# A ViT tower with attention, two scans and two quantised feed-forward layers on one core: products on the PE array that nobody reads, in ten waits of a turn and at its end

## Time and profile before

| | |
|---|---|
| median of 3 runs | 2763.31 us (2760.47 to 2763.85) |
| the profiled execution | 2761.31 us |
| its span, first to last instruction | 2759.5 us |
| mean granted PE clock | 0.877 of full speed |
| PE busy | 2064.6 us, 75% of the span |
| DVE busy | 2064.4 us, 75% |
| ACT busy | 1289.5 us, 47% |
| POOL busy | 1263.9 us, 46% |
| first q product of the turns | at 47.4, 724.89, 1399.56 and 2080.82 us |

### The profile page before, as it was taken

The page is one execution under the profiler, slowest core; times in us unless marked ns, Lnnn a source line. Parts: engine busy times, 40 slices in busy tenths (PEclk is TensorE's granted clock), DMA queues, the critical chain, the costliest instruction groups (busy, mean ns, idle before and its releaser), DMA issues.

```text
span 2759.5 us, 23184 instructions
## 1 busy us (share of the span) xinstructions
PE 2064.6 (75%) x8068; PEld 1131.9 (41%) x8068; DVE 2064.4 (75%) x2361; ACT 1289.5 (47%) x1822; POOL 1263.9 (46%) x615
## 2 busy tenths in 40 slices
PE   3977776677797777778689687676858968767785
PEld 1225652235422665224532275422443236632253
DVE  6844869986783587997778257899687827789967
ACT  1563356553164436654326443665323644456632
POOL 2130249991213126997222311799521231289932
PEclk9898898999799987989779888899987989779997
DMA  7300000000520000000061000000006100000000
GB/s 182 75 12 0 1 0 0 0 0 1 89 59 1 0 1 0 0 0 0 1 101 47 1 1 1 0 0 0 0 1 112 36 0 1 0 0 0 0 0 16
DMA packets 40558, 51.36 MB, mean 19 GB/s; under 512 B 8560, under 2 KB 31856, under 8 KB 40432
## 3 DMA queue, kind: packets, MB, share of 16 engines
q1 hardware_dynamic: 40432, 49.75, 8.5%
HBM read 26.25 MB, written 10.49 MB: 13 GB/s over the span
## 4 chain that ended last, share of the span: by engine, by line
PE 47%; DVE 23%; POOL 14%; issue 9%; ACT 5%; DMA 1%; SPq 0%; POOLq 0%; DVEq 0%; ACTq 0%
PE psum L621 14%; PE psum L849 10%; POOL big L1608 9%; PE psum L735 4%; PE psum L710 4%; POOL big L1597 4%; PE psum L723 3%; DVE mid L1183 3%; DVE mid L1412 3%; PE psum L679 2%; PE psum L745 2%; PE psum L668 2%; DVE big L1229 2%; ACT mid L907 2%; PE psum L631 2%
## 5 line engine op out<-in xcount | busy, mean ns | idle before, releaser
L849 PE MATMUL psum<-big,ident 128*128 128x512 f32 x992 | 530.1, 684 | 190.5 <-POOL big L1608 190.2
L1478 DVE TENSOR_TENSOR_SCAN big<-psum,b,big 128x512 f32<-128x512 f32 x512 | 614.0, 1261 | 0.0
L907 ACT ACTIVATE big<-psum 128x1024 f32<-128x1024 f32 (+2 forms) x592 | 452.4, 776 | 338.4 <-PE psum L723 204.2
L1608 POOL TENSOR_TENSOR big<-big 128x2048 f32<-128x2048 f32 x124 | 560.5, 4520 | 22.2 <-DVE big L1478 22.2
L907 ACT ACTIVATE psum<-mid,aneg 128x512 f32<-128x512 f32 x512 | 353.9, 692 | 265.0 <-DVE big L1478 265.0
L849 PEld LDWEIGHTS psum<-big,ident 128*128 128x128 f32 x992 | 205.0, 217 | 474.2 <-POOL big L1608 252.1
L1283 DVE TENSOR_REDUCE negmax<-psum 128x1 f32<-128x512 f32 x512 | 317.5, 679 | 16.6 <-PE psum L710 16.3
L1597 POOL TENSOR_TENSOR big<-mid,big 128x512 f32<-128x512 f32 (+1 forms) x128 | 223.4, 1745 | 19.9 <-ACT big L907 19.9
L710 PE MATMUL psum<-mid 96*128 96x512 bf16 x512 | 214.9, 423 | 22.8 <-DVE nm_rows L1299 13.2
L1551 POOL TENSOR_TENSOR lsum<-lsum,onorm 128x512 f32<-128x512 f32 x32 | 40.5, 1266 | 408.3 <-ACT onorm L907 408.3
L907 ACT ACTIVATE mid<-mid 128x513 f32<-128x513 f32 (+2 forms) x112 | 97.9, 899 | 227.0 <-DVE mid L1169 226.8
(11 more groups left out here) (168 smaller groups left out, 3359.8 us busy)
## 6 DMA issues: line engine op xcount, KB each, us to landing
mid<-mid SPq DMA_DIRECT2D x96, 128.0 KB, 8.8
mid<-scratch SPq DMA_DIRECT2D x192, 64.0 KB, 2.3
scratch<-big SPq DMA_DIRECT2D x4, 1536.0 KB, 14.4
out<-hres SPq DMA_DIRECT2D x8, 513.0 KB, 7.5
big<-in_x SPq DMA_DIRECT2D x8, 512.0 KB, 4.1
big<-in_w SPq DMA_DIRECT2D x2, 1024.0 KB, 6.4
mid<-nm_rows SPq DMA_DIRECT2D x96, 4.0 KB, 1.7
big<-in_wg SPq DMA_DIRECT2D x1, 1024.0 KB, 9.7
```

The lines of the kernel that those rows point to most:

```text
L849: mm = nc.tensor.matmul(y_psum[:, c], ident[:, :], st(1, k)[:, c], start=(n == 0), stop=(n == NS - 1))
L907: return nc.scalar.activation(o, a, func, **kw)
L1478: V.tensor_tensor_scan(st(0, k)[:, c], a_psum(DT * k + c), st(0, k)[:, c], b0[:, p, n, c:c + 1], ALU.mult, ALU.add).then_inc(scanned, 1)
L1608: G.tensor_tensor(st(1, k), st(0, k), c_row(k).unsqueeze(1).broadcast_to([P, DT, S]), ALU.mult).then_inc(hc_ready, 1)
```

## The change

Three constants say how many products are put in each place. `keep_busy` issues n products of `w1` by itself (128 rows, 128 columns of weights, 512 bf16 columns) into a PSUM region whose previous content has been read and whose next content is written from scratch by PE; nobody reads them and they raise no semaphore. `warm` first waits for the slot of the fill that comes next and then does that in the slot. The places, in the order of a turn: in `project` before the wait on POOL for p = 1 (32; the wait for the unit is moved ahead for that); before the affine wait (20); before T0 of p = 0 (12); in quantiser 1 before I1 of p = 0 (10), T1 of p = 1 (14) and I1 of p = 1 (6); before the d fills of layer norm 3 (8); before T2 of p = 0 (12); in quantiser 3 the same three as in quantiser 1; and at the turn's end, ahead of the waits of L899, behind a wait for DVE's reading of the first y fill (8). That is 152 a turn.

```diff
--- before.py
+++ after.py
@@ -67,6 +67,11 @@
 POOL_G = (0, 2, 3, 5, 6)
 PE_CONV = (1, 2, 4, 7)
 CONV_LAG = 3
+
+
+WARM = {"affine": 20, "T0": 12, "I1_0": 10, "T1_1": 14, "I1_1": 6, "LN3": 8, "T2": 12, "I3_0": 10, "T3_1": 14, "I3_1": 6}
+WARM_O = 32
+WARM_END = 8
 
 
 def tile_count(shared, p, c):
@@ -622,6 +627,15 @@
                                                   stop=(n == len(products) - 1))
                     mm.then_inc(full[FILLS[name, p][0]], 1)
 
+                def keep_busy(o, n):
+
+                    for _ in range(n):
+                        nc.tensor.matmul(o, w1[:, 0, 0:P], w1[:, 0, 0:BANK], start=True, stop=True)
+
+                def warm(name, p, n):
+                    slot_free(name, p)
+                    keep_busy(flat_slot(name, p), n)
+
                 def convolve(p, c):
 
                     slot_free(f"v{c}c", p)
@@ -651,6 +665,10 @@
                 def token_maxima(q, pairs=range(PAIR)):
 
                     for p in pairs:
+                        if q % 2 == 0 and p == 0:
+                            warm(f"T{q}", p, WARM[f"T{q}"])
+                        elif q % 2 and p == 1:
+                            warm(f"T{q}", p, WARM[f"T{q}_1"])
                         pe.wait_ge(absmax_part, q_of(q, p))
                         slot_free(f"T{q}", p)
                         for c, (t0, n) in enumerate(CHUNKS):
@@ -660,6 +678,8 @@
                 def token_rows(q, pairs=range(PAIR)):
 
                     for p in pairs:
+                        if q % 2:
+                            warm(f"I{q}", p, WARM[f"I{q}_{p}"])
                         for name, which, step in (("I", 2, q_inverse(q, p)), ("S", 3, q_step(q, p, Q_STEPS[q]))):
                             pe.wait_ge(q_scale, step)
                             slot_free(f"{name}{q}", p)
@@ -739,8 +759,10 @@
 
                 def project(p, c):
 
+                    unit_ready(("O", p, c))
+                    if (p, c) == (1, 0):
+                        keep_busy(unit(("O", p, c)), WARM_O)
                     pe.wait_ge(o_normed, NG * (p + 1))
-                    unit_ready(("O", p, c))
                     for g in range(NG):
                         mm = nc.tensor.matmul(unit(("O", p, c)), wo[:, g, c * P:(c + 1) * P], onorm[:, g],
                                               start=(g == 0), stop=(g == NG - 1))
@@ -771,6 +793,7 @@
                 pe.wait_ge(o_copied, NGRP)
 
                 layer_norm(0, lambda p: hres[:, p])
+                warm("a0", 0, WARM["affine"])
                 for p in range(PAIR):
                     pe.wait_ge(affine, 2 * p + 2)
                     for name, wt in (("a", wa), ("u", wB)):
@@ -803,6 +826,7 @@
                     for c in range(KT):
                         fill(f"g{c}", p, [(w2[:, k, c * P:(c + 1) * P], mid_bf(p, 5, HT)[:, k]) for k in range(HT)])
                 layer_norm(3, lambda p: hres[:, p])
+                warm("d0", 0, WARM["LN3"])
                 for p in range(PAIR):
                     pe.wait_ge(ln_normed, q_of(3, p))
                     for c in range(DT):
@@ -896,6 +920,8 @@
                     pe.wait_ge(q_ready, q_of(3, p))
                     for c in range(KT):
                         fill(f"y{c}", p, [(wd[:, k, c * P:(c + 1) * P], mid_bf(p, 5, HT)[:, k]) for k in range(HT)])
+                pe.wait_ge(res_scaled, 2 * PAIR + 1)
+                keep_busy(flat_slot("y0", 0), WARM_END)
                 for s in range(4):
                     pe.wait_ge(full[s], NFILL[s])
                 pe.drain().then_inc(pe_done, 1)
```

## The result

Timed on the same chips in 20 runs each, the changed kernel takes 2749.93 us (median; 2738.58 to 2765.40) and the one before 2761.31 us (2758.14 to 2768.25). The ratio of the two is 0.9965, with a 95% interval of 0.9954 to 0.9976 (written [0.9954, 0.9976] from here on). That is 9.7 us less; the two medians by themselves lie 11.4 us apart. The forecast was 2747. The profiled execution took 2754.95 us, 5 us above its kernel's median, and its span is only 6.4 us shorter than before's 2759.5 us. What follows accounts for these 6.4 us.

A forecast was written before the change was run, and what follows sets the result against it. No engine bounds the whole; PE, DVE and POOL alternate, so only PE clock lost on the chain can be won. Terms 4.3+4.6+6.0+6.8+6.6-5.9-6.0 give 16.4 us less: 2744.9, plus 2 for the median, 2747; range 2729 to 2768.

The forecast's parts named there:

- case A: Whole kernel: the sum of all terms, 16.4 us less, 2747 us, own range 2738 to 2755; chance 0.40.
- The third layer norm: Eight products before the d fills leave 0.8 us idle; the whole 6.8 us is gained, at worst 0.
- a stage on the chain gives its time to the end: Third layer norm: DVE's next work waits for these products, so the stage's 6.8 us counted as whole-kernel gain.
- Rows, POOL and DVE: Quantisers 1 and 3: earlier rows of p = 1 let POOL overlap DVE's multiply less; 6.6 us gained, at most 8.8.
- The second halves of g and y: They wait for DVE after 4 to 5 us idle and run slower; 5.9 us lost, between 0 and 12.3.
- The turn's end: Eight products ahead of PE's return to the loop's head delay three next turns by 2 us each; 6.0 lost.
- Projection and affine: Before both stages: 32 and 20 products gain 4.3 and 4.6 us; clock drops taken at two in three and one in two.
- T0 and T2, 12 each: Quantiser transposes: 2.2 us idle left, 0.75 us gained a place, 6.0 in all, between 0 and 22.5.
- Rival B: T0 and T2: the transposes' stages give nothing, as transposes do not count as busy PE; 2753 us, chance 0.15.
- Rival D: Turn's end: PE's return costs up to 3.5 us each at three ends, slower overall; 2777 us, chance 0.14.

The follow-up runs named there:

- e1: Kernel before plus only the eight products before the third layer norm's d fills: ratio 0.9999 to the kernel before, 2759.70 us.
- e9: Changed kernel with long waits filled further, also between halves of g and y and before the scan's last sum, none at turn's end: 0.9797, 2704.35 us.
- e12: e9 without the ten products before the d fills of layer norm 3: ratio 0.9834 to the kernel before, 2713.93 us.
- e3: Kernel before plus only the products inside quantisers 1 and 3 (10, 14 and 6): ratio 0.9957 to the kernel before, 2747.34 us.
- e4: Changed kernel without the eight products at the turn's end and their wait: ratio 0.9938 to the kernel before, 2747.29 us.
- e6: Changed kernel with 16 more products between the first and second half of g and of y: ratio 0.9926 to the kernel before, 2737.50 us.
- e7: Changed kernel with 44 instead of 32 products before the projection and 28 instead of 20 before affine: ratio 0.9904 to the kernel before, 2732.18 us.
- e5: Changed kernel with 20 products instead of 12 before T0 and before T2: ratio 0.9862 to the kernel before, 2722.25 us.
- e2: Kernel before plus only the eight products at the turn's end: ratio 1.0018 to the kernel before, 2766.30 us.
- e10: Kernel before plus three unread 128x512 DVE multiplies a turn after layer norm 3: ratio 1.0048 to the kernel before, 2773.31 us.

## Why the prediction was right, and where not

**The sum.** The forecast was 16.4 us less, 9.7 were measured, and the two profiles differ by only 6.4. The sign and the leading case A were right; the size was too large by two thirds. Luck had a part in how near 2747 is to 2749.93: the three runs behind the forecast had their median 2 us higher than the twenty. The range of 2729 to 2768 also held the kernel before, so that lying in it proves little. What speaks for the reasoning are the terms, one by one:

**The third layer norm** (6.8 forecast): 6.76 in the stage, clock 1.00, as worked out. As a gain of the whole kernel it was not there when it stood alone (e1), and was 9.6 us within e9 (e12). The step "a stage on the chain gives its time to the end" lacks that other stages' losses move with it.

**Rows, POOL and DVE** (6.6): 8.1, since all eight places came through and not three in four. The multiply was forecast at 3.3 us and took 3.30, and e3 isolates it. That slow rows make POOL late, and POOL's overlap holds DVE up, was the right reading of the earlier trace rows. The Trainium skill (GPSIMD Engine Reference, section on specifications) says that GpSimd shares its way into SBUF with VectorE where that one has two SBUF inputs; multiplies of 2.85 us without overlap, 3.30 with 0.6 us of it and 4.42 with 1.7 agree.

**The second halves of g and y** (5.9 lost): 3.6 at g and 2.8 at y, 6.4 in the stages. By themselves the slow halves of y would be covered (e4 against before); with the end products behind them they are not (the changed kernel against e6).

**The turn's end** (6.0 lost): 5.5 by e4 against the changed kernel, 1.8 a switch. The products do stand ahead of PE's own return, as was said, but they cost their full length only because the second half of y is slow; behind a fast one the switch is 10.1 to 10.8 us (e6). The prediction charged both terms in full, though a part of each is covered. From the start of y's second half on, 5.4 us were lost in all (45.3 to 50.7).

**Projection and affine** (4.3 and 4.6): 1.9 and 3.0. The chances were too kind: the clock fell after 3.38 us in four of four, not two in three, and after 2.53 in three of four, not in half. Each fall costs one piece of 1.7 us, as assumed (e7: 9.68 to 7.98 us, 36.06 to 34.45). The step failed in its odds, not in its mechanism.

**T0 and T2, 12 each** (6.0): this is the term that failed. I gave them 0.75 us a place although the rest is 2.2 us and the work behind it thin, and together they cost 0.3. After such a rest the clock was lost in seven of eight places, and the stage's 9.0 to 12.1 us were as bad as before. Rival B had the number for this term, though not the reason: in e5 the same transposes keep the full clock once the wait before them is filled further. Eight more products in each of these places take 21.7 us out of the two stages (85.2 to 63.5), more than the whole change does.

**Not forecast at all**: +2.3 in attention, +3.2 in the scan's last sums, -1.5 after G. None of these stages has an edit. A like deal shows in every profile of these runs, with either sign. Which turn loses its clock at which wait these rows don't tell, and what decides it stays open; filling the waits (e9) took most of it away. Rival D, PE's return as the bound, had the mechanism in part and the size wrong: y's slow half and the end products together cost some 1.8 us a switch and not 3.5, and the rows' gain was there.

## What to carry to other kernels

Where idle time in front of an engine's work costs it its clock, fill the wait until under one microsecond is left, or leave it: in the three long waits here, half to two thirds filled gave little, and the rest gave most of the gain. Look first at the waits ahead of thin work, keep such filling away from a loop's end where the engine's own return is on the path, and ask what stage comes next, since work that is done sooner may wait longer. Before two costs at one place are added, ask whether one covers the other. When a clock is dealt anew at every shift, judge a piece by its stage in the profile and a version by timed runs of the whole, and expect the sum of single runs to be too high.

## What the runs showed of the hardware

- **How long a rest may be.** With rests of 0.4 to 0.9 us no drop was seen at any of these places. At some 2.2 us (T0, T2 with 12 products; changed kernel, e4, e6, e7) the stage was above 7.94 us in 25 of 32 cases; at 2.5 us (affine; changed kernel, e4, e5, e6) above 34.5 in 13 of 16; at 3.4 us (projection, the same four) above 7.98 in 14 of 16; at 2.56 us (layer norm 3 without products; before, e2, e3, e10, e12) the stage stood at its longer time in 18 of 20. The same rest in the same place goes both ways, so within 2 to 3.5 us its length alone does not decide.
- **1.93 us can be too much.** g's first half took 3.69 us after 1.94 of rest in e9, 5.33 after 1.93 in e12, and 5.35 in all four turns of e6.
- **When one stage moves by under 2 us a turn, losses elsewhere move too, and by more.** e1: 6.7 us gained in the stage and at most some 1 in the timed whole, though its profiled execution kept all 7; e12: 5.1 lost in the stage and 9.6 in the whole.
- **PE's start of a turn.** It lies 9.8 to 10.6 us after the start of y's second half in the kernel before and in e4 (8.4 to 11.1 in all runs without products there), whether that half takes 3.7 us or 5.4. With eight products behind a half of 5.4 it is 11.6 to 11.9 (changed kernel), behind one of 3.7 only 10.1 to 10.8 (e6). What holds PE there no row names ("issue"), and it was not tried to shorten it.
